# Output projection from float32r halves made on GpSimd, and x1's rounding constant taken off on GpSimd

## What is computed

```python
x = layernorm(x + attention(x))        # 16 heads of 16; w_q, w_k, w_v, w_o ternary, with scales and biases
x = layernorm(x + ffn(x))              # width 704
# ffn: fp4_linear(silu(fp4_linear(x, w_gate)) * fp4_linear(x, w_up), w_down)
# fp4_linear quantises both operands: blocks of 16 along the last axis, scale = max|x| / 6,
# each value to the nearest of 0, .5, 1, 1.5, 2, 3, 4, 6 times its scale
```

## Time and profile before

| | |
|---|---|
| median of 3 runs | 1953.61 us (1952.48 to 1954.31) |
| the profiled execution | 1955.24 us, its span 1953.4 us |
| mean granted TensorE clock | 0.998 |
| busy: TensorE, VectorE, ScalarE, GpSimd | 1922.9, 1828.6, 1641.7, 918.3 us |
| first stage, attention, feed-forward (about) | 0 to 190, 190 to 1410, 1410 to 1953 us |
| HBM read and written | 103.68 and 73.40 MB |

### The profile page before, as it was taken

One profiled execution on the slowest core, in us unless ns is written; L12 is line 12 of the kernel. 1 busy time (PEld: TensorE's weight loads), 2 busy tenths in 40 slices (PEclk: granted clock), 3 DMA queues, 4 the chain that ended last, 5 costly groups with the idle time before them and its releaser, 6 DMA issues.

```text
span 1953.4 us, 43156 instructions
## 1 busy us (share of the span) xinstructions
PE 1922.9 (98%) x15934; PEld 1112.8 (57%) x15934; DVE 1828.6 (94%) x3087; ACT 1641.7 (84%) x3225; POOL 918.3 (47%) x779
## 2 busy tenths in 40 slices
PE   8999999999999999999999999999999999999998
PEld 7776444444444444444444444444478888888876
DVE  4799999999999999999999999998299999999997
ACT  6655999999999999999999999998867777777776
POOL 3000446675776665365122122212156666666785
PEclk9999999999999999999999999999999999999999
DMA  7985633444354445435434543542111111111200
GB/s 225 303 262 211 116 56 47 84 89 106 77 106 90 90 94 100 95 78 103 96 85 94 101 95 78 103 96 85 40 36 49 49 50 49 49 50 55 66 30 28
DMA packets 127199, 181.47 MB, mean 93 GB/s; under 512 B 37836, under 2 KB 82636, under 8 KB 126988
## 3 DMA queue, kind: packets, MB, share of 16 engines
q1 hardware_dynamic: 119308, 171.10, 36.8%
q10 hardware_dynamic: 7392, 7.34, 1.2%
q0 software_dynamic: 288, 0.27, 0.1%
HBM read 103.68 MB, written 73.40 MB: 91 GB/s over the span
## 4 chain that ended last, share of the span: by engine, by line
DVE 63%; PE 33%; issue 2%; ACT 1%; DMA 0%; DVEq 0%; SPq 0%; POOLq 0%; POOL 0%; ACTq 0%
DVE halfmax L1154 43%; DVE halfmax L1149 14%; PE ps L1430 10%; PE ps L1469 6%; PE ps L505 4%; PE ps L517 2%; PE ps L1418 2%; PE ps L1441 2%; PE ps L1064 2%; PE ps L1030 1%; PE ps L492 1%; PE ps L1477 1%; DVE room L1620 1%; PE ps L476 1%; PE ps L1486 1%
## 5 line engine op out<-in xcount | busy, mean ns | idle before, releaser
L1115 ACT ACTIVATE room<-ps 128x512 f32<-128x512 f32 x2048 | 1086.1, 599 | 106.4 <-PE ps L1030 80.4
L1154 DVE TENSOR_REDUCE halfmax<-ps 128x1 f32<-128x512 f32 x1470 | 901.2, 678 | 0.0
L1030 PE MATMUL ps<-qs,ks 50*128 50x512 f32 x2048 | 718.9, 449 | 2.6 <-DVE halfmax L1154 1.2
L1005 PE MATMUL ps<-ks,qs 48*128 48x512 f32 x1960 | 678.7, 439 | 4.8
L1064 PE MATMUL ps<-room,vals 128*17 128x256 f32 (+2 forms) x8192 | 578.7, 384 | 0.2 <-ACT craw L1123 0.2
L1005 PEld LDWEIGHTS ps<-ks,qs 48*128 48x128 f32 x1960 | 311.4, 184 | 407.0 <-DVE halfmax L1154 250.0
L1030 PEld LDWEIGHTS ps<-qs,ks 50*128 50x128 f32 x2048 | 325.1, 184 | 19.9 <-ACT room L1115 14.1
L1064 PEld LDWEIGHTS ps<-room,vals 128*17 128x17 f32 x8192 | 167.5, 96 | 251.4 <-issue 187.9
L1149 DVE TENSOR_REDUCE halfmax<-ps 128x2 f32<-128x1024 f32 x245 | 296.3, 1209 | 0.9 <-PE ps L1005 0.8
L164 POOL CAST mrow<-turned_rows 128x32 fp32r<-128x32 f32 x32 | 6.7, 210 | 576.0 <-DVE turned_rows L159 576.0
L1430 PE MATMUL ps<-wguT,xqT 128*128 128x512 f32 (+1 forms) x1152 | 266.8, 384 | 3.9 <-DVE xqT L1660 3.9
(11 more groups left out here) (120 smaller groups left out, 2266.6 us busy)
## 6 DMA issues: line engine op xcount, KB each, us to landing
qk_parts<-parts SPq DMA_DIRECT2D x64, 512.0 KB, 5.4
qs<-qk_parts SPq DMA_DIRECT2D x192, 128.0 KB, 4.3
ks<-qk_parts SPq DMA_DIRECT2D x192, 128.0 KB, 6.7
ctx_raw<-craw SPq DMA_DIRECT2D x64, 256.0 KB
ready<-passing SPq DMA_DIRECT2D x27, 512.0 KB, 4.8
pairs<-ready SPq DMA_DIRECT2D x27, 512.0 KB
out_dram<-fin SPq DMA_DIRECT2D x64, 128.0 KB, 1.9
xin<-in_L_attn_x_dram ACTq DMA_DIRECT2D x14, 512.0 KB, 6.8
```

What stands on the lines that cost most here:

```text
L1005: nc.tensor.matmul(ps[:, MX + max_number(i, u, bank) % 4, :], qs[rows, i.slot(RING), pair, t * P:(t + 1) * P], ks[rows, i.slot(RING), pair ...
L1030: nc.tensor.matmul(ps[:, score_bank(i, s, n), :], ks[rows, slot, pair, kt * P:(kt + 1) * P], qs[rows, slot, pair, qh * BANK:(qh + 1) * BAN ...
L1115: nc.scalar.activation(prob[:, prob_slot(i, s), score_order(i, s)[n], :], ps[:, score_bank(i, s, n), :], ACT.Exp, scale=float(D) ** -0.5). ...
L1154: nc.vector.tensor_reduce(halfmax[:, i.slot(2), bank, column:column + 1], ps[:, at + bank, :], AX.X, ALU.max, negate=True).then_inc(max_re ...
```

## The change

- w_o is kept twice: as float32 (`wT`) and, new, as a high and a low float32r half (`wo_half`; ScalarE copies, VectorE splits).
- In `pass_pair` GpSimd also makes a high float32r copy of the multiplied context and the low rest (`passing_half`). The halves go to `ready`, x with bias to a DRAM tensor of its own, `plus_dram`. `pass_pair` is called after three of the six quantising steps of a group and no longer right behind the maxima.
- For the tiles below `RAW` the output projection is three float32r products of two matmuls (`PRODUCTS`), six in all, and no longer two float32 matmuls. Tiles from `RAW` on stay with float32.
- The raw context and sums of the last pairs have two buffers of their own (`passing` and the new `late`) and are loaded one pair ahead (`load_late`); their x is loaded two pairs ahead as before.
- In the feed-forward the subtraction of the constant on x1's grid is GpSimd's, right before its scale; VectorE waits before x1's division until the grid of the tile before is made.

The diff, its core:

```diff
@@ sync of attend
         def store_passing(p):
-            sp.wait_ge(passing_ready, 2 * (p + 1))
-            sp.dma_start(ready_dram[p].rearrange("p (a c n) -> p a c n", a=2, c=HC), passing[:, 0:2]
+            sp.wait_ge(passing_ready, 4 * (p + 1))
+            sp.dma_start(ready_dram[p].rearrange("p (a c n) -> p a c n", a=2, c=HC), passing_half[:, :].bitcast(F32)
                          ).then_inc(passing_stored, 16)
+            sp.dma_start(plus_dram[p].rearrange("p (j h) -> p j h", j=2), passing[:, 1]).then_inc(passing_stored, 16)
@@ gpsimd of attend
             pool.wait_ge(fq_chain, n[0])
+            if n[0] % FQ_PER_GROUP == FQ_PER_GROUP // 2:
+                next_pair()
             if n[0] % FQ_PER_GROUP == 0:
                 next_maxima()
...
             last.then_inc(passing_ready, 1)
+            pool.wait_ge(passing_ready, 4 * p + 1)
+            wait(pool, passing_stored, 32 * p)
+            nc.gpsimd.tensor_copy(passing_half[:, 0], passing[:, 0]).then_inc(passing_ready, 1)
+            pool.wait_ge(passing_ready, 4 * p + 3)
+            nc.gpsimd.tensor_tensor(passing_half[:, 1], passing[:, 0], passing_half[:, 0].bitcast(F32),
+                                    ALU.subtract).then_inc(passing_ready, 1)
@@ sync of feed
+        def load_late(p):
...
+            if p >= READY + 2:
+                sp.wait_ge(sems["wo_psum"], 2 * p - 2)
+            load_raw(sp, p, ctx_dram, rden_dram, *raws[p % 2], raw_in[p % 2])
...
+            if i.k % 2 == 0 and READY <= i.k // 2 + 1 and i.plus(2).ok(NT):
+                load_late(i.k // 2 + 1)
@@ output_projection
             for c in cs:
-                last = nc.tensor.matmul(ps[:, WO, 0:H], pairs[:, pair % PAIRS, 0, c, half * P:(half + 1) * P], wT[:, 1, c, :],
-                                        start=c == 0, stop=c == HC - 1)
+                if t.k >= RAW:
+                    last = nc.tensor.matmul(ps[:, WO, 0:H], raws[pair % 2][0][:, c, tokens], wT[:, c, :],
+                                            start=c == 0, stop=c == HC - 1)
+                    continue
+                for n, (a, b) in enumerate(PRODUCTS):
+                    last = nc.tensor.matmul(ps[:, WO, 0:H], pairs[:, pair % PAIRS, a, c, tokens], wo_half[:, b, c, :],
+                                            start=n == 0 and c == 0, stop=n == len(PRODUCTS) - 1 and c == HC - 1)
@@ vector of feed
             if on2:
+                due(dve, "xgrid_ready", t2.lin(1))
                 gx.divide().then_inc(sems["xn_ready"], 1)
...
                 gx.add("xm_ready").then_inc(sems["xsum_ready"], 1)
-                due(dve, "xsum_ready", t2.lin(1, 1))
-                due(dve, "xq_ready", t2.lin(1))
-                nc.vector.tensor_tensor(xg[:, :], xn[:, :], xm[:, :],
-                                        ALU.subtract).then_inc(sems["xgrid_ready"], 1)
@@ gpsimd of feed
             t = i.plus(-2)
             if t.ok(NT):
+                due(pool, "xsum_ready", t.lin(1, 1))
+                nc.gpsimd.tensor_tensor(xg[:, :], xn[:, :], xm[:, :], ALU.subtract).then_inc(sems["xgrid_ready"], 1)
                 due(pool, "xgrid_ready", t.lin(1, 1))
@@ project: copy_weights and split_weights for w_o
+            if m == 3:
+                nc.scalar.activation(wT[:, :, :], ps[:, w_bank(m), :].rearrange("p (c o) -> p c o", c=HC), ACT.Copy)
-            dst = (wqk[:, 0, 0], wqk[:, 0, 1], wv[:, 0], wT[:, 1])[m]
+            dst = (wqk[:, 0, 0], wqk[:, 0, 1], wv[:, 0], wo_half[:, 0])[m]
...
+            if i.k == 1:
+                split_weights(3)
```

More of the change, by code:

```diff
@@ L194, in build @@
         ident = sb("ident", [P, P])
-        wT = sb("wT", [P, 2, HC, H])
+        wT = sb("wT", [P, HC, H])
+        wo_half = sb("wo_half", [P, 2, HC, H], F32R)
         s_all = sb("s_all", [P, 4])
@@ L244, in build @@
         passing = sb("passing", [P, 3, HC, 2 * P])
-        pairs = sb("pairs", [P, PAIRS, 3, HC, 2 * P])
+        pairs = sb("pairs", [P, PAIRS, 2, HC, 2 * P], F32R)
+        plus = sb("plus", [P, PAIRS, 2, H])
         wguT = sb("wguT", [P, 2, HC, 2 * I], F32R)
@@ L252, in build @@
         spare = sb("spare", [P, 1])
+        passing_half = sb("passing_half", [P, 2, HC, 2 * P], F32R)
+        late = sb("late", [P, 2, HC, 2 * P])
+        raws = ((passing[:, 0], passing[:, 2]), (late[:, 0], late[:, 1]))
+        raw_in = [sem(f"raw_in{j}") for j in range(2)]
         third = feed(nc, sem, room, fq, buffers, x_tok, ctx_dram, rden_dram, out_tok, ps, ident, wT, s_all, b_row,
                      wguT, wd, wdT, wt_psum, wt_ready, wt_split, numbers, sums, craw_ready, craw_stored, rden_ready, rden_stored,
-                     ready_dram, pairs, pair_in, passing_stored)
+                     ready_dram, plus_dram, pairs, plus, raws, raw_in, pair_in, passing_stored, wo_half)
         with ExitStack() as inner:
@@ L632, in split_weights @@
             dve.wait_ge(wT_ready, m + 1)
-            high, low = (wqk[:, part, m] if m < 2 else wv[:, part] for part in range(2))
+            high, low = (wqk[:, part, m] if m < 2 else (wv, wo_half)[m - 2][:, part] for part in range(2))
             nc.vector.tensor_tensor(low, ps[:, w_bank(m), :].rearrange("p (c o) -> p c o", c=HC),
@@ L1655, in vector @@
                 nc.vector.scalar_tensor_tensor(out=y[:, :], in0=ps[:, WO, 0:H], scalar=s_all[:, 3:4],
-                                               in1=pairs[:, pair % PAIRS, 1, half], op0=ALU.mult,
+                                               in1=plus[:, pair % PAIRS, half], op0=ALU.mult,
                                                op1=ALU.add).then_inc(sems["wo_used"], 1)
@@ L1731, in gpsimd @@
                 pool.wait_ge(pair_in[pair % PAIRS], pair_loads(pair))
-                raw, rcp = (pairs[:, pair % PAIRS, part, :, half * P:(half + 1) * P] for part in (0, 2))
+                pool.wait_ge(raw_in[pair % 2], 64 * ((pair - READY) // 2 + 1))
+                raw, rcp = (part[:, :, half * P:(half + 1) * P] for part in raws[pair % 2])
                 nc.gpsimd.tensor_tensor(raw, raw, rcp, ALU.mult).then_inc(sems["ctx_ready"], 1)
-                with_b = pairs[:, pair % PAIRS, 1, half]
+                with_b = plus[:, pair % PAIRS, half]
                 nc.gpsimd.tensor_tensor(with_b, with_b, b_row[:, 1], ALU.add).then_inc(sems["xb_ready"], 1)
```

59 lines of the change are left out of this document (34 added, 25 removed).

## The result

| | before | after |
|---|---|---|
| median | 1953.96 us (6 runs, 1952.48 to 1956.71) | 1966.49 us (6 runs, 1964.59 to 1967.41) |
| ratio, 95% interval | | 1.0064 (1.0054 to 1.0074): slower, by 0.64% |
| span of the profiled execution | 1953.4 | 1965.5 |
| y of tile 2 (L1655, after L1703) starts at | 1410.6 | 1411.1 |
| tiles 2 to 53 | 417.0 | 423.5 |

What follows compares the result with a forecast made beforehand. VectorE was taken to bound the attention and last ten tiles, TensorE the feed-forward between. Projection -1.4 and -0.5, last tiles -0.8, the rest 0: -2.7 us, median 1950.9; range 1943.5 to 1956.5, the forecast's own 1948.5 to 1953.5.

Steps and rivals of the forecast that it cites:

- The projection: Output projection, 54 tiles: float32r frees TensorE of 0.16 us a tile; -1.4 us for the pairs, -0.5 around them.
- The wait for hT: Feed-forward: TensorE's x1 transposes wait for ScalarE's hT copy, so only 0.06 us a pair of the saving counts.
- The constant on x1's grid: Feed-forward, all 64 tiles: VectorE loses 0.43 us a tile, GpSimd gains a product of 0.62; no effect in steady state.
- Cost 0: Feed-forward: GpSimd's added subtraction fits into its waiting time and later results are not needed sooner; 0 us.
- the port's price: Feed-forward: VectorE's rounding of h is slowed beside GpSimd's products, 0.4 us per us, +0.3 a tile, hidden under TensorE.
- Rival (c): Feed-forward: VectorE's rounding of h waits for both GpSimd products; +12.9 and +7.1 us, 1973.1; chance 0.10 together with another rival.
- The last ten tiles: Tiles with raw context: VectorE 8.48, GpSimd 8.41 to 8.7; 8.53 us each instead of 8.61, together -0.8 us.
- late loads: Last ten tiles: raw context loaded one pair ahead, issued 17 us before the multiply, lands in time; 0 us.
- Attention, first stage, stores of the halves: Attention: GpSimd's 2.5 us a group and the extra store, 0, at most +0.5 a tight group; first phase 0 to +0.3.
- the list in the prediction: Expected feed-forward signs: transposes waiting for hT in both tiles, a pair at 16.3 us, GpSimd's wait before hg shrinking but remaining.

Runs made afterwards that it cites:

- experiment 1: The changed kernel with the subtraction of the constant on x1's grid back on VectorE: 1951.55 us, ratio 0.9989.
- experiment 9: The kernel of experiment 1 with both hT copies on ScalarE moved before x1's normalisation: 1948.42 us, ratio 0.9967.
- experiment 2: The kernel before with only the subtraction of the constant on x1's grid moved to GpSimd: 1963.88 us, ratio 1.0052.
- experiment 8: The changed kernel with ScalarE's copy of hT's last pieces moved before x1's normalisation: 1966.24 us, ratio 1.0069.
- experiment 7: The kernel of experiment 1 with ScalarE's copy of hT's last pieces moved before x1's normalisation: 1955.03 us, ratio 1.0006.

## Why the prediction was wrong

**The projection: right.** -1.4 us for the pairs and -0.5 around them; experiment 1 gives -2.1 us, and 0.065 us a pair where 0.06 stood. The 0.5 cannot be told by itself: the start of the feed-forward varies by more from one profiled execution to another. The wait for hT was read rightly as what eats the saving; experiment 9 frees it.

**The constant on x1's grid: the step that failed.** "Cost 0" rested on two sentences. One: L1752 "started at 1710.33 anyway after waiting 0.83", so that 0.6 us more would fit in. The length of the queue was nearly right: L1790 takes 0.68. But L1793 takes 1.15 instead of 0.62, since it waits for L1675's end, and hg starts 0.44 us behind L1675 instead of 0.08. The other: "hq is read at the end of TensorE's next iteration", so that its lateness costs nothing. For TensorE that is so. But VectorE's scale, in the middle of its iteration, waits for hq through the port, and this closes a loop over VectorE, ScalarE and GpSimd, of 8.03 us before and 8.33 after, that the prediction did not look for. Put at 0, the subtraction cost 10.2 us alone (experiment 2) and 14.9 beside the new projection (from experiment 1 to the changed kernel). I looked for the port's price at L1627 alone, and only as a slowing of 0.4 us per us. It is an exclusion: L1627's 1.02 us are 0.27 of waiting for L1745 and 0.75 behind it. L1598's two durations, 0.21 and 0.47 us, were in the trace of before and said so.

**The port's rule.** The page of the Trainium skill named in the prediction (SBUF — State Buffer, Who interferes with whom) gave the right behaviour (whole instructions exclude each other), as the scale's ends show, and I set the weaker reading above it. Rival (c) drew on it but put it at the wrong place: it priced L1627's wait for both products, at 19.5 us, with 1.88 us as the point where it decides. L1675 took 1.10. The loss came from the waits of xq and the scale, 12.5 us in all, and these stood in no rival: the port was the right suspect, at the wrong instructions.

**The last ten tiles.** 8.53 us each were forecast, 9.04 measured (90.4 / 10): GpSimd's 8.4 to 8.7 left out both scale and L1668 waiting for it. Experiment 2, without late loads, takes 90.9 us too, so they are not the cause; that they came in time is as forecast.

**Attention, first stage, stores of the halves: right**, at nothing; the maxima were in time with 25 us more work on GpSimd.

**What would have shown it.** Of the list in the prediction: L1534 does start 0.14 to 0.15 us behind the copy of hT in both tiles of a pair, but the pair is at 16.66 and not 16.3 us; and the waits of L1752 (L1800 after), expected to shrink, are nearly gone, 4.2 us in all, in 2 of 63 tiles, instead of 54.8. That is the sign that hg, and hq behind it, is late.

## What to carry to other kernels

Before work is put on GpSimd, list what GpSimd will do later because of it, and which VectorE instructions will then stand beside it. Here those with two SBUF operands, and tensor_scalar with one, waited for the end of the whole GpSimd product, however small they were themselves, and no semaphore shows it. Reductions and statistics from SBUF and instructions with an operand in PSUM did not wait (L1614 on h takes 0.89 us beside hg in each tile, L1655 0.47 to 0.48 beside hq). Then follow such waits around: idle time of GpSimd is usable only where nothing behind it in the queue is pushed onto an instruction that waits for it, on a loop that is nearly as long as the bound. And where an engine is relieved, look for who it waits for next: here 0.16 us a tile on TensorE was worth 0.03 until ScalarE's copies were moved ahead.

## What was not expected of the hardware

- The exclusion is whole and exact: each scale shown that starts beside hq ends 0.05 to 0.08 us behind it, and a 60-column instruction of 0.21 us took up to 0.83.
- Not every GpSimd instruction holds VectorE back: where the scale starts together with GpSimd's one-column power (L1724, 0.61 to 0.62 us), as four times in the kernel before, it takes 0.21 us as alone and ends 0.4 us before it.
- A GpSimd fill that reads nothing takes 0.32 us for 128x256, half of what a product of 256 columns takes (0.62).
- The granted clock was 0.83 and 0.65 in 1350 to 1360 and 1360 to 1365 us in the profiled execution of before, 0.81 and 0.70 in that of after, and 1.00 in both stretches in experiment 1. There y of tile 2 starts at 1406.8, 3.8 us earlier than before. The clock is not the whole of it: with 1.00 from 1350 to 1410 us that start is at 1405.4 in experiment 8 and at 1409.1 in experiment 7. So stages are to be compared by their own length. What sets it off was not tried.
